# Where a tile's batches and steps change places: from the relu and the low half to the second adjacency product

## The reference, cut to what matters

```python
# first network (L0)
h = relu(einsum('ts,bsh->bth', adj, x @ Wg0 + bg0))
h = relu(einsum('ts,bsh->bth', adj, h @ Wg1 + bg1))
for p in 1, 2, 3, 4:             # an LSTM over windows of p steps of h
    h[:, idx, :] = last state of each window
x = layernorm(x + h)
# second network (L1): graph attention over 256 edges, then
x = layernorm(x + attention(x))
```

## Time and profile before

| | us |
|---|---|
| median of 3 runs | 981.24 (980.89 to 982.06) |
| the profiled execution | 980.76 |
| its span | 979.0 |
| TensorE busy in it | 907.4 |
| VectorE, ScalarE, GpSimd busy | 695.2, 637.1, 211.6 |

### The profile page before, as it was taken

The page is one execution under the profiler, slowest core; times in us unless marked ns, Lnnn a source line. Parts: engine busy times, 40 slices in busy tenths (PEclk is TensorE's granted clock), DMA queues, the critical chain, the costliest instruction groups (busy, mean ns, idle before and its releaser), DMA issues. The chain is left out here.

```text
span 979.0 us, 15308 instructions
## 1 busy us (share of the span) xinstructions
PE 907.4 (93%) x5551; PEld 777.5 (79%) x5551; DVE 695.2 (71%) x1379; ACT 637.1 (65%) x1171; POOL 211.6 (22%) x567
## 2 busy tenths in 40 slices
PE   5999999999999999999999999946877999999895
PEld 5999977667778789999988878835666888888684
DVE  5656558998777777777777777745555787786674
ACT  3546469997767776676667566625776667676354
POOL 1000000000000000000000000025765666666665
PEclk9999999999999999999999999977999999999998
DMA  6131200000000000000000000011111122221122
GB/s 188 44 87 56 74 1 0 1 1 1 0 1 1 1 1 1 1 1 1 1 1 1 1 0 1 1 51 33 44 44 33 45 65 66 66 66 33 44 66 65
DMA packets 55537, 29.09 MB, mean 30 GB/s; under 512 B 2625, under 2 KB 55206, under 8 KB 55462
## 3 DMA queue, kind: packets, MB, share of 16 engines
q1 hardware_dynamic: 52294, 26.01, 9.2%
q10 hardware_dynamic: 2848, 1.05, 0.4%
q0 software_dynamic: 320, 1.05, 0.3%
HBM read 19.72 MB, written 8.39 MB: 29 GB/s over the span
## 5 line engine op out<-in xcount | busy, mean ns | idle before, releaser
L350 ACT ACTIVATE work<-psum,bias 128x512 f32<-128x512 f32 (+1 forms) x504 | 295.4, 645 | 31.8 <-PE psum L302 30.9
L283 PE MATMUL psum<-hT_hi,w_hi 128*128 128x512 f32 (+1 forms) x504 | 189.9, 377 | 7.2 <-ACT work L350 4.8
L284 PE MATMUL psum<-hT_lo,w_hi 128*128 128x512 f32 (+1 forms) x504 | 185.9, 369 | 0.0
L285 PE MATMUL psum<-hT_hi,w_lo 128*128 128x512 f32 (+1 forms) x504 | 185.0, 367 | 0.0
L338 ACT ACTIVATE work<-work 128x512 f32<-128x512 f32 (+1 forms) x144 | 85.6, 594 | 103.2 <-DVE work L466 68.9
L663 POOL MEMSET a_wide<- 128x60 f32 x1 | 0.1, 148 | 641.8 <-POOLq L88 641.8
L474 DVE TENSOR_TENSOR work<-work 128x512 f32<-128x512 f32 (+1 forms) x144 | 90.5, 628 | 55.6 <-ACT work L338 55.6
L283 PEld LDWEIGHTS psum<-hT_hi,w_hi 128*128 128x128 f32 x504 | 95.2, 189 | 33.7 <-ACT work L350 17.4
L459 DVE TENSOR_TENSOR work<-work 128x512 f32<-128x512 f32 (+1 forms) x144 | 90.1, 625 | 25.0 <-ACT work L350 25.0
L285 PEld LDWEIGHTS psum<-hT_hi,w_lo 128*128 128x128 f32 x504 | 95.3, 189 | 15.5
L284 PEld LDWEIGHTS psum<-hT_lo,w_hi 128*128 128x128 f32 x504 | 95.2, 189 | 13.3
(11 more groups left out here) (171 smaller groups left out, 1707.6 us busy)
## 6 DMA issues: line engine op xcount, KB each, us to landing
work<-x SPq DMA_DIRECT2D x32, 256.0 KB, 3.2
x_res<-x SPq DMA_DIRECT2D x32, 256.0 KB, 2.9
out<-x_kept SPq DMA_DIRECT2D x32, 256.0 KB, 2.3
work<-L_gnn_Whh ACTq DMA_DIRECT2D x4, 256.0 KB, 5.8
work<-L_gnn_Wih POOLq DMA_DIRECT2D x4, 256.0 KB, 9.5
work<-L_gnn_bg SPq DMA_DIRECT2D x5, 32.5 KB
x_kept<-L_gnn_src SPq DMA_DIRECT2D x1, 128.0 KB, 3.7
x_kept<-L_gnn_dst SPq DMA_DIRECT2D x1, 128.0 KB, 3.8
```

The costliest lines, as they stand in the source:

```text
L283: pe.matmul(out, wh, xh, start=True, stop=False)
L284: pe.matmul(out, wh, xl, start=False, stop=False)
L285: mm = pe.matmul(out, wl, xh, start=False, stop=(t == 0))
L350: op = act.activation(gate[s][g][:, 0:ph.width], psum[:, 4 * s + g, 0:ph.width], ACT.Tanh if g == G else ACT.Sigmoid, bias=bias[:, b:b + 1])
```

## The change

TensorE's L253 writes each batch's 128 columns at a step of four elements, so that bank 2s is in the order `(t b)` from there on. All that follows is flat: L325 and L421 are as they were, L258 to L263 compute in `(t b)`, and relu and low half lose their `by_batch` views. For the bias product of L258 the row sums have to stand in the same order, so `deg_rows` becomes `[RANKS, P, BT]`; it is written at a step of four elements in the setup, and L244 reads its weights at that step.

```diff
-        deg_rows = sb("deg_rows", [RANKS, BT, P], F32R)
+        deg_rows = sb("deg_rows", [RANKS, P, BT], F32R)
...
-        def batches_of(flat):
-            return flat.rearrange("p (b t) -> p b t", b=BT)
...
-                    pe.matmul(out, deg_rows[:, 0, :], bg0_rows[:, :, :], start=True, stop=False, skip_group_check=True)
+                    pe.matmul(out, deg_rows[:, :, 0], bg0_rows[:, :, :], start=True, stop=False, skip_group_check=True)
...
-                        mm = pe.matmul(psum[:, 2 * s, b * P:(b + 1) * P], h1[s][:, b, :], adjT[:, :], start=True, stop=True)
+                        mm = pe.matmul(by_batch(psum[:, 2 * s, :])[:, b, :], h1[s][:, b, :], adjT[:, :], start=True, stop=True)
...
-                    act.activation(by_batch(hT_hi[:, cols]), batches_of(psum[:, 2 * s + 1, :]), ACT.Relu).then_inc(h2_hi, 1)
+                    act.activation(hT_hi[:, cols], psum[:, 2 * s + 1, :], ACT.Relu).then_inc(h2_hi, 1)
...
-                op = dve.tensor_copy(deg_rows[:, b, :], psum[0:RANKS, 1, 0:P])
+                op = dve.tensor_copy(deg_rows[:, :, b], psum[0:RANKS, 1, 0:P])
...
-                op = dve.tensor_tensor(deg_rows[lo, b, :], psum[lo, 1, 0:P], deg_rows[lo, b, :].bitcast(F32), ALU.subtract)
+                op = dve.tensor_tensor(deg_rows[lo, :, b], psum[lo, 1, 0:P], deg_rows[lo, :, b].bitcast(F32), ALU.subtract)
...
-                    dve.scalar_tensor_tensor(out=by_batch(hT_lo[:, cols]), in0=batches_of(psum[:, 2 * s + 1, :]), scalar=0.0,
-                                             in1=by_batch(hT_hi[:, cols].bitcast(F32)), op0=ALU.max,
+                    dve.scalar_tensor_tensor(out=hT_lo[:, cols], in0=psum[:, 2 * s + 1, :], scalar=0.0,
+                                             in1=hT_hi[:, cols].bitcast(F32), op0=ALU.max,
                                              op1=ALU.subtract).then_inc(h2_done, 1)
```

## The result

The changed kernel takes 984.31 us (median of 20 runs, 982.4 to 986.06), the kernel before 982.24 us (median of 20, 980.47 to 983.9): ratio 1.0022, 95% interval 1.0015 to 1.0029. It is slower by 2.1 us, on the other side of the forecast, which was 1.2 us faster; whether it lies beyond "within 0.2%" is open, since the interval holds 1.002. No rival had this case as its own: rival 3 held the right place and half the size.

What follows compares the result with a forecast made beforehand. TensorE was taken to bound the GNN stage, with ScalarE and VectorE exposed only at its end. The terms -0.97 - 0.2 + 0 + 0 + 0 made -1.2 us, so 979.9 us, range 978.8 to 1010.5.

Steps and rivals of the forecast that it cites:

- rival 3: Small exposed costs, stepped L244 weights (up to +2.0 us) or 1 to 2 ns per L253 store: 980.5 to 982; chance 0.08.
- Weights of L244: Bias product's weight load at a step of 16 bytes, 32 times: bounds 0 to +2.0 us, taken as 0.
- rival 1: TensorE's stepped PSUM writing at L253 runs at half pace in all eight iterations: about 1008 us; chance 0.36, 0.40 with variants.
- two signs of a wrong forecast: GNN stage ends over 1 us later than 140.6, or any stage behind 150 us changes length by over 1 us.
- The end of the stage: Last iteration, where TensorE waits for relu and low half: L283 starts at 142.01 instead of 142.98, -0.97 us.
- The setup's eight stepped writes: Copies and subtractions into `deg_rows`: 0.8 us of VectorE, covered by its 5.06 us idle time, so cost 0.
- Rival 2: Relu and low half: the stride was not their cost, so the end keeps its 2.38 us gap: 981.2; chance 0.04.
- The second adjacency product: L253's 256 instructions writing PSUM at 16-byte steps: bounds 0 to +51 us, taken as 0.
- The clock: Behind the gap at the GNN stage's end: a shorter gap may avoid the half-clock drop, 0 to -0.41 us, taken -0.2.
- the prediction's +0.5: Profiled execution of the kernel before, 980.76 us, taken as 0.48 us under the median of the runs, 981.24.

Runs made afterwards that it cites:

- e2: Kernel before with only the bias product's (L244) weights read at a step of 16 bytes: 985.73 us against 981.92, ratio 1.0035.
- e5: Kernel before with only the bias product's (L244) weights read at a step of 8 bytes: 982.23 us against 982.12, ratio 1.0.
- e7: Changed kernel with the four bias products of an iteration issued in a row: 981.43 us against 982.12 for the kernel before, ratio 0.9995.
- e4: Changed kernel with h1 and adjT of the second adjacency product in bfloat16, stored in one pass at a step of 16 bytes: 971.2 us, one run.
- e3: Kernel before with h1 and adjT of the second adjacency product in bfloat16, stored flat in one pass: 967.51 us, one run.
- e6: Kernel before with only the bias product's (L244) weights read at a step of 32 bytes: 987.38 us, a single run.
- e1: Changed kernel with the bias product's weights read from a flat copy: 980.42 us against 981.92 for the kernel before, ratio 0.9983.
- e8: As e4, with the second adjacency product's columns stored at a step of 8 bytes instead of 16: 970.47 us, one run.

## Why the prediction was wrong

**What failed** is the term "Weights of L244". It gave bounds of 0 to +2.0 us and took 0; it measured +3.8 to +4.1 us (e2), about 0.12 us on each of 32 loads. Two steps of it were wrong.

- The price was carried over from L728, a transpose. There the step adds 207 - 144 = 63 ns to 128 values. In L244's load it adds 314 - 192 = 122 ns, about 0.95 ns a value, twice as much. The rows held the warning: flat, the same 128 values take 192 ns in a product and 144 in a transpose, so the two loads were not of one kind, and the transposing one should not have given the upper end. VectorE's 0.79 ns a value, which the text had beside it, would have given 0.10 us x 32 = +3.2.
- The cover was judged by a total, not by an addition: the +15 ns of a load like L728's "would still be under the neighbour matmul". But loads of 192 ns follow each other every 0.1116 us, so a load's duration is more than the time that it takes from the pace, and the product ahead gives only 0.11 us. Nothing was left under it: the full 0.12 us came out, 32 times. Even 6 ns come out: in e5, with 198 ns, the first and the fourth of an iteration's bias products stand 70.00 - 66.60 = 3.40 us apart, before 70.45 - 67.07 = 3.38, which is 7 ns for each of the three distances, and so in every iteration but the first. e7 puts 512-column products (0.23 us) ahead of three of the four loads, and three of the four costs go.

So the sum was -1.2 where the same sum with +3.9 gives +2.7, and the medians say +2.1. The range reached over it only because of rival 1, whose mechanism is not the one at work, and "slower" was given for the wrong reason. That the measured time lies in the range is luck. Rival 3 named the right place with a chance of 0.08 and called it small. (Rival 1's own price takes off the 1.2 us twice: 979.9 + 28.6 and + 32 are 1008.5 and 1011.9, not 1007.3 and 1011. Nothing measured hangs on it.)

Of the two signs of a wrong forecast, the first came true and pointed at the right stage: the last product before the gap ends at 145.66 - 1.41 = 144.25 us, not within 1 us of 140.6. The second came true without a cause: behind the first transpose of the second network a stage is 1.5 us longer, with no edit in it.

**What held.** The GNN stage is bound by TensorE, and the time taken off ScalarE and VectorE in iterations 1 to 7 is worth nothing. The end of the stage gained 0.97 us as worked out. The setup's eight stepped writes went from 279 to 374 and from 276 to 369 ns, 0.75 us of durations and 0.50 us on the clock since they overlap, and VectorE still idles for 3.58 us behind them (5.06 in the earlier trace rows). Rival 2 is out: stride was the whole difference of relu and low half.

**The second adjacency product** was taken as free, and is free. The reason given fits: an estimated 0.87 ns from one column address to the next in plain float32, while the stepped store of e4 takes 0.107 us for 128 columns, 0.84 ns each. e3 and e4 make that more than the 4 ns it was inferred from: if an instruction wrote its 128 columns twice, one time behind the other, it would take 2 x 0.107 = 0.21 us; it takes 0.1116, flat and stepped. Rival 1, with 0.40 in all, described a real property of the store at a product that doesn't meet it. What goes on inside an instruction is not shown; the paces are.

**The clock** term had the right sign, was too small for this pair, and its cause was wrong. From the first gate product to the first transpose of the second network it is 505.69 us before and 505.18 in the changed kernel, 0.5 less where -0.2 was taken and -0.41 was the bound, and the drop at the LSTMs' start is gone. But the gap's length alone doesn't decide it. e2 keeps the 2.35 us gap and has the full clock, as these windows show (140 to 160 us; clock third from the end), of before, e2 and the changed kernel:

```profile
140.00:160.00 20.00, 17.62 (x69) 13.81 (x68) 14.58 (x25) 17.24 (x29) 0.00 (x0) 0.91 0.00 1
```

```profile
140.00:160.00 20.00, 17.65 (x75) 13.07 (x75) 14.05 (x23) 17.02 (x27) 0.00 (x0) 1.00 0.00 1
```

```profile
140.00:160.00 20.00, 18.59 (x80) 13.81 (x79) 13.78 (x24) 16.49 (x29) 0.00 (x0) 1.00 0.00 1
```

e6, with a gap of 2.37 us, shows 0.91 as well, and so does e3 with 2.39 (120 to 140 us there); e5 with 2.36 shows 1.00. So three of five executions with the long gap dropped, and none of the five with 1.41 us (changed, e1, e4, e7, e8). What the drop costs is the same both times: 505.69 and 505.71 us in before and e6, 505.14 to 505.18 in e1, e2, e5, e7 and the changed kernel. What decides it at a gap of 2.4 us stays open. The start of the second network scatters as well; 650 to 690 us, before and then changed:

```profile
650.00:690.00 40.00, 25.09 (x157) 21.02 (x158) 21.58 (x76) 16.65 (x34) 18.35 (x52) 0.76 0.17 47
```

```profile
650.00:690.00 40.00, 24.65 (x140) 20.55 (x140) 19.79 (x71) 13.94 (x29) 18.11 (x46) 0.66 0.19 51
```

From its first transpose to the end it is 330.3 us before, 331.9 changed and 330.8 (e7) to 332.4 (e6) in e1, e2 and e5 to e7, without an edit there. The profiled execution of before was thus a quick one, 1.5 us under the median of the 20 runs, and the prediction's +0.5 for that was too little. A difference of spans of 1 or 2 us between two profiles of this kernel says nothing unless it is located in a stage.

## What to carry to other kernels

When a layout change moves a stride from one engine to another, list every operand that gets the stride, the small ones too: here the large stepped store was free and the 65 x 128 weights cost 3.9 us, where the rest of the change gained 1.5. Price a weight load by a load of the same kind, and take as its cover the pace of the product ahead of it (0.11 us for 128 columns, 0.23 for 512), not its duration. On a bound engine, read the distance from start to start; the idle column stayed at zero here when a weight load got longer.

## What was not expected of the hardware

- A stepped weight load costs 0.95 ns a value in a float32r product (314 against 192 ns) and 0.49 ns in a transpose (207 against 144), at the same step and 128 values. For the product's load the edge lies between 8 and 16 bytes: 198 and 313 ns.
- TensorE's store into PSUM at a step of 8 or of 16 bytes runs a one-pass bfloat16 product of 128 columns at 0.107 us instead of 0.061 (one execution each), while plain float32 products of the same shape keep 0.1116 us with and without the step.
